# Hybrid attention, mixture-of-experts and linear-attention kernel: two steps of the first attention stage moved, both attention stages' layer loops written out

## The chip, the core and the metric

The kernel runs on one core of one Trainium2 chip. The metric is the device time of one execution in microseconds. Before the change it was 3831.24 us, the median of three runs (3824.48 to 3834.24).

## What the kernel computes

The input `x` has 8 sequences of 512 tokens with 128 channels, all in float32. Four stages follow one another, each applied to the normalised `x` and added to it:

```python
x = x + attn_a(layernorm(x))   # 16 heads of 64
x = x + ffn(layernorm(x))      # router, 16 experts of which 8 count per token, one shared expert
x = x + attn_b(layernorm(x))   # a transformer of 6 layers, 16 heads of 8, linear attention
x = x + ffn(layernorm(x))
```

Only `attn_a` and `attn_b` are touched. `attn_a`, cut to what matters:

```python
# per head; SK is a running sum of outer products that begins at eye * sqrt(64)
SK = cumsum(outer(kk, vk)) + SK_state
y  = q @ (SK / (norm(SK) + 1e-8)).T          # the new query
scores = rotary(y) @ rotary(k).T / 8         # causal, softmax over 512 keys
out = softmax(scores) @ v ; return concat_heads(out) @ w_out + b_out
```

`attn_b` runs six layers of projections, exponential feature maps, causal linear attention, an output projection, layer norm, a feed-forward of 512 and a second layer norm.

## The kernel before

Everything stays on chip: `x` is one tile of 128 partitions by 8 x 512. In the attention stage a "layer" is one of 8 pairs of heads; within a layer the 8 sequences go through one after the other. Work on a sequence is a list of named steps, and three sequences are in flight at once: one comes in (projections, states, the new query), one is mixed (scores, softmax, weighing), one goes out. A *slot* is one turn of this pipeline: all steps of `AttentionPlan.SLOT` (line 216), once. `LEAD` and `FIRST` are shorter lists that fill the pipeline, `TAIL` and `END` empty it.

Each engine walks the same slots by the function `pipeline` (line 168) and issues only what it has to do in each step. TensorE and GpSimd take the order of `SLOT`; ScalarE and VectorE have orders of their own (`ACT`, `DVE`, lines 218 and 219). Each engine executes its queue strictly in order. Between engines there are counters: a matmul group that fills a PSUM bank raises `filled[bank]`, the engine that has read it raises `emptied[bank]`. `FILLS` (line 220) says which banks a step fills; `Slot.fill` computes from the order of the steps which count a wait must reach. There are eight banks: a0, a1, a2 for the incoming sequence, s0, s1 for scores, t0, t1 for turned probabilities, z for the weighed sum.

The steps that matter here, with TensorE's line and who reads the result:

- P0, P3 (line 445): projections of q and vk, of k and kk, into a0 and a1; ScalarE copies them (lines 622, 632).
- P1, P2 (line 445 too, as 128x384): the token projections of chunks 0 and 1 (banks a2, a0) and 2 and 3 (a1, a2). ScalarE copies them to `tok[parity_in]` (line 627). This buffer also holds the values which W3 of the same slot reads.
- L0, L1 (line 485): linear scores of the first and the second half, into a0 and a1; VectorE masks them (line 692). L1 needs P3's banks, so ScalarE's copies of `k_own` and `kkT`, to be done.
- St (line 500): the state products, into a2; VectorE adds them up (line 702), after its part of S2.
- Yi (line 511) needs VectorE's masked scores, Ys (line 518) the added states; then ScalarE copies y (line 636), VectorE forms `zk` and its running sum, and `inc` (line 527) multiplies with it. `inc` is TensorE's last step of a slot.
- S0 to S3 (lines 557, 561): scores of query chunk c; VectorE takes the maximum, ScalarE the exponential (line 658).
- T0 to T3 (line 577): turn the probabilities; ScalarE copies them (line 647). W0 to W3 (line 590): weigh the values with them into bank z.
- `inv` (line 535) and `outs` (line 544): turned reciprocals, and the output projection.

The transformer stage is built in the same way from `TransformerPlan`, with slots that begin with the turn of `o` (line 1019) and end with S1, 64 small matmuls (line 977).

The layers run in a loop. `e.Fori` emits its body once and jumps back at its end; inside, counts to wait for depend on the layer, so they are computed by register instructions. The attention stage loops over 7 of its 8 layers and the transformer over 5 of its 6; the last layer is emitted by itself. SyncE's own loop of the transformer's weight loads, and the loops of the `ffn` stages, are separate.

Of the kernel before, what the change touches and what calls it, by code (L numbers as in the profile page):

```python
# [134 lines left out]
def fills(plan, steps, bank):  # L135

    return sum(plan.FILLS[step].split().count(bank) for step in steps)


class Slot:  # L140
# [20 lines left out]
    def fill(self, bank, step):  # L161

        plan = self.plan
        n = sum(fills(plan, p, bank) for p in self.passed) + fills(plan, self.steps[:self.steps.index(step)], bank)
        return self.slots * fills(plan, plan.SLOT, bank) + n


def pipeline(e, plan, weights_in, weights_out, body, order=None):

    def run(slot, sequence):
        for step in slot.steps if order is None else [step for step in order if plan.joins(step, slot.steps)]:
            if step != "weights":
                body(step, slot, sequence)
            elif slot.build is not None:
                weights_in(slot.build, slot)

    B, once = plan.B, [plan.LEAD, plan.FIRST]  # L180
    weights_in(0, None)
    run(Slot(plan, plan.LEAD, [], 0, 0, 0, 0, new_weights=True), {"in": 0, "next": 1})
    run(Slot(plan, plan.FIRST, once[:1], 0, 0, 0, 0), {"in": 1, "next": 2})

    def layer(l, final):
        g = l * B

        def slot(z, parity, **more):
            return Slot(plan, plan.SLOT, once, g + (z - 1), g + z, l, parity, **more)

        weights_out(l, slot(1, 1, final=final))
        for z in range(1, B - 2):
            run(slot(z, z % 2), {"in": z + 1, "next": z + 2, "out": z - 1})
        run(slot(B - 2, 0, build=None if final else l + 1), {"in": B - 1, "next": B, "out": B - 3})
        if final:
            run(Slot(plan, plan.TAIL, once, g + (B - 2), g + (B - 1), l, 1), {"out": B - 2})
            run(Slot(plan, plan.END, once + [plan.TAIL], g + (B - 2), g + B, l, 0), {"out": B - 1})
        else:
            run(slot(B - 1, 1, new_weights=True), {"in": 0, "next": 1, "out": B - 2})
            run(slot(B, 0), {"in": 1, "next": 2, "out": B - 1})  # L200

    with e.Fori(0, plan.LAYERS - 1) as l:
        layer(l, False)
    layer(plan.LAYERS - 1, True)


def sequence_of(tokens, z):
# [3 lines left out]
class AttentionPlan:  # L211
# [1 line left out]

    SLOT = ("P0 T3 S0 W3 P1 inv P2 S1 L0 outs T0 P3 weights T1 L1 Xn S2 St W0 W1 Yi Ys T2 S3 W2 inc").split()
    LEAD = "X P0 P1 P2 L0 P3 L1 Xn St Yi Ys inc".split()
    ACT = "P0 T3 S0 P1 inv P2 S1 T0 P3 T1 S2 Ys T2 S3".split()
    DVE = "W3 S0 inv S1 L0 outs P3 weights L1 S2 St Ys S3 inc rot scale".split()
# [1 line left out]
                 Ys="a0 a1", inc="a2", inv="t0", outs="a2", T0="t0", weights="", T1="t1", T2="t0 t1", T3="t0 t1",  # L221
# [4 lines left out]
    END = "T3 W3 inv outs".split()  # L226
    FIRST = [step for step in SLOT if step not in ("T3", "W3", "inv", "outs")]
    TAIL = [step for step in SLOT if step[0] in "STWio" and step not in ("St", "inc")]

# [5 lines left out]
def attention_block(nc, mem, ins, B):  # L235
# [12 lines left out]
    plan = AttentionPlan()  # L248
    plan.B, plan.LAYERS = B, PAIRS
    with ExitStack() as ctx:  # L250
# [3 lines left out]
        def sem(name):  # L254
            return ctx.enter_context(nc.semaphore("a_" + name))
# [41 lines left out]
        filled = {k: sem("filled_" + k) for k in plan.BANKS}  # L297
# [14 lines left out]
        def wait(e, name, slot, n):  # L312

            e.wait_ge(s[name], slot.of(PHASE[name]) * EVENTS[name] + (n + 1))

        def wait_filled(e, bank, slot, step):
            e.wait_ge(filled[bank], slot.fill(bank, step) + 2)
# [9 lines left out]
        def wait_staged(e, hp, slot, step=None):  # L327

            e.wait_ge(w_loaded, (hp + 1) * 16)
            if slot is not None:  # L330
                for bank in ("a0", "a1", "a2"):
                    e.wait_ge(filled[bank], slot.fill(bank, step or slot.steps[0]) + 1)
            e.nop(nofuse=True)
# [4 lines left out]
        with nc.Block() as block:  # L338
            @block.sync
            def _(sp):  # L340
# [20 lines left out]
                def body(step, slot, sequence):  # L361
# [3 lines left out]
                    elif step == "Ys":  # L365
                        wait_emptied(sp, "a0", slot, "Ys")
                        swap(y_swap, y_own, s["y_swapped"])

                pipeline(sp, plan, weights_in, weights_out, body)
                sp.wait_ge(mem["rest_loaded"], mem["rest_loads"])  # L370
                sp.wait_ge(w_loaded, PAIRS * 16)
# [51 lines left out]
            def _(pe):  # L423
# [9 lines left out]
                def body(step, slot, sequence):  # L433
# [147 lines left out]
                    elif step[0] == "W":  # L581
# [13 lines left out]
                        if c == TILES - 1:  # L595
                            t.then_inc(filled["z"], 1)

                pipeline(pe, plan, weights_in, weights_out, body)

            @block.scalar  # L600
            def _(act):
                for k in plan.BANKS:
                    act.sem_inc(emptied[k], 1)
                act.sem_inc(made_out, 1)

                def weights_in(hp, slot):
                    pass

                def weights_out(hp, slot):
                    wait_staged(act, hp, slot)  # L610
                    nc.scalar.copy(w_o[:], staged[:, 5 * P:6 * P]).then_inc(made_out, 1)
                    act.wait_ge(made_out, hp + 2)
                    act.nop(nofuse=True)

                def body(step, slot, sequence):
                    def full(bank):
                        wait_filled(act, bank, slot, step)

                    if step == "P0":
                        for n in range(2):  # L620
                            full(f"a{n}")
                            nc.scalar.copy(qv[:, :, n, :], ps[f"a{n}"].rearrange("p (c n) -> p c n", c=TILES)
                                           ).then_inc(emptied[f"a{n}"], 1)
                    elif step in ("P1", "P2"):
                        for n, bank in enumerate(plan.FILLS[step].split()):
                            full(bank)
                            nc.scalar.copy(tok[slot.parity_in][:, 2 * (step == "P2") + n, :],
                                           ps[bank][:, 0:3 * P]).then_inc(emptied[bank], 1)
                    elif step == "P3":
                        for dst, bank in ((k_own, "a0"), (kkT, "a1")):  # L630
                            full(bank)
                            nc.scalar.copy(dst[:], ps[bank]).then_inc(emptied[bank], 1)
                    elif step == "Ys":
                        full("a0")
                        full("a1")
                        nc.scalar.copy(y_own[:].rearrange("p (c n) -> p c n", c=TILES), yz[:, :, 0, :]
                                       ).then_inc(emptied["a0"], 1)
                    elif step == "inv":
                        full("t0")
                        nc.scalar.copy(inv_rows[:], ps["t0"][:]).then_inc(emptied["t0"], 1)  # L640
                    elif step[0] == "T":
                        c = int(step[1])
                        n, banks = (c + 1) * P, plan.FILLS[step].split()
                        for i, bank in enumerate(banks):
                            hs = slice(0, 2) if len(banks) == 1 else slice(i, i + 1)
                            full(bank)
                            nc.scalar.copy(probT[c % 2][:, hs, 0:n],  # L647
                                           ps[bank][:, 0:2 * n // len(banks)].rearrange("p (h n) -> p h n", n=n)
                                           ).then_inc(emptied[bank], 1)
                    elif step[0] == "S":  # L650
                        c = int(step[1])
                        wait(act, "shifts", slot, c + 1)
                        if c == 0:
                            act.wait_ge(s["inv"], slot.of("mix") + 1)
                            act.nop(nofuse=True)
                        for h in range(2):
                            k = 2 * c + h
                            nc.scalar.activation(prob[c % 2][h][:, 0:(c + 1) * P], ps[f"s{h}"][:, 0:(c + 1) * P],  # L658
                                                 ACT.Exp, bias=shift[:, k:k + 1], scale=scale[slot.parity][:, k:k + 1],
                                                 accum_out=row_sum[:, k:k + 1]).then_inc(emptied[f"s{h}"], 1)  # L660

                pipeline(act, plan, weights_in, weights_out, body, plan.ACT)

            @block.vector
# [94 lines left out]
class TransformerPlan:  # L759


    SLOT = ("turn att project values Wo mapq A1 mapk h1 keys weights F1 sums S0 F2 nums A0 S1").split()
    LEAD = "turn project values mapq mapk keys sums S0 A0 S1".split()
# [6 lines left out]
                 S0="s0 s1 s2 s3", S1="s0 s1 s2 s3", A0="n0", A1="n1",  # L770
# [1055 lines left out]
```

## Time and profile before

| | |
|---|---|
| median of 3 runs | 3831.24 us (3824.48 to 3834.24) |
| the profiled execution's own time | 3831.35 us |
| its span, first to last instruction | 3829.6 us |
| instructions | 103815 |
| TensorE matmuls busy | 3485.5 us, 91% |
| TensorE weight loads busy | 2723.9 us, 71% |
| VectorE busy | 2636.2 us, 69% |
| ScalarE busy | 1703.6 us, 44% |
| GpSimd busy | 901.5 us, 24% |
| mean granted TensorE clock | 0.972 |

The attention stage lies between about 50 and 1600 us, the transformer stage between about 1980 and 3460 us; the two `ffn` stages follow them. A busy share is the time in which an engine had an instruction in work. In a row of waits, "A <- B" says that the engine named first stood idle until B released it; "issue" stands for idle time in which it waited for nothing that the profile shows. Matmul durations overlap, so the step from start to start counts, not the sum of durations.

### The profile page before, as it was taken

Reading aid. Unit: us, or ns where it says so; the run is one execution under the profiler, and the core shown is the slowest. Engines: PE = TensorE matmul, PEld = TensorE weight load, DVE = VectorE, ACT = ScalarE, POOL = GpSimd, SP = SyncE. Lnnn points to the kernel's source line nnn. Section 1 sums busy time; section 2 is a strip of 40 time slices with the busy share of each in tenths; the row PEclk is TensorE's granted clock in tenths of the full one; section 3 lists DMA queues with packets and bytes.
Section 4 is the critical chain, followed back from the end, with each engine's and each line's share of the span. In section 5 each row is a group of like instructions: output and inputs, shape, how many; then the busy total and the mean of one; then the engine's idle time right before and its main releaser. Section 6 shows DMA issues by size and latency. Waiting matters only on the chain. (4 is left out here: it accounts for less than half of the span.)

```text
span 3829.6 us, 103815 instructions
## 1 busy us (share of the span) xinstructions
PE 3485.5 (91%) x39640; PEld 2723.9 (71%) x39640; DVE 2636.2 (69%) x6838; ACT 1703.6 (44%) x3438; POOL 901.5 (24%) x781
## 2 busy tenths in 40 slices
PE   4999999999999999799958999999999999987998
PEld 3767676767676777688846777777777777756887
DVE  3565655555655555588866778878888788867787
ACT  2555555555555555433323444444434444422332
POOL 3232323232323232100001332232223222320000
PEclk9999999999999999899979999999999999988999
DMA  3000000000000000000000000000000000000000
GB/s 88 29 24 28 24 28 24 28 24 28 24 28 24 28 23 23 12 1 0 1 14 16 2 16 2 2 16 2 16 3 2 16 2 3 2 2 1 1 0 22
DMA packets 38420, 60.41 MB, mean 16 GB/s; under 512 B 6960, under 2 KB 16688, under 8 KB 37552
## 3 DMA queue, kind: packets, MB, share of 16 engines
q1 hardware_dynamic: 37936, 53.78, 4.3%
q8 instruction: 326, 5.34, 0.6%
q14 instruction: 158, 1.29, 0.1%
HBM read 18.10 MB, written 2.10 MB: 5 GB/s over the span
## 5 line engine op out<-in xcount | busy, mean ns | idle before, releaser
L658 ACT ACTIVATE a_prob<-a_s,a_shift,a_scale 128x128 f32<-128x128 f32 (+3 forms) x512 | 311.5, 612 | 483.6 <-DVE a_shift L741 483.4
L1538 ACT ACTIVATE ffn_silu<-ffn_ps_g 128x512 f32<-128x512 f32 x272 | 161.2, 599 | 382.5 <-PE ffn_ps_g L1488 370.2
L1481 PEld LDWEIGHTS ffn_ps_y<-moe_down,ffn_hidden 128*128 128x128 f32 x2176 | 282.1, 191 | 40.0 <-issue 18.5
L1481 PE MATMUL ffn_ps_y<-moe_down,ffn_hidden 128*128 128x128 f32 x2176 | 288.1, 275 | 16.0 <-DVE ffn_acc L1642 16.0
L940 POOL TENSOR_TENSOR t_rstd<-t_var_eps,minus_half 128x4 f32<-128x4 f32 x96 | 97.7, 1017 | 834.9 <-DVE t_var_eps L1252 834.9
L1190 ACT COPY t_num<-t_n 128x512 f32<-128x512 f32 x96 | 56.2, 585 | 515.4 <-PE t_n L1001 514.8
L1642 DVE SCALAR_TENSOR_TENSOR ffn_acc<-ffn_ps_y,ffn_combine,ffn_acc 128x128 f32<-128x128 f32 x960 | 270.5, 347 | 7.7
L1654 DVE TENSOR_TENSOR ffn_hidden<-ffn_silu,ffn_ps_u 128x512 f32<-128x512 f32 x272 | 186.1, 686 | 106.5 <-ACT ffn_silu L1538 74.5
L409 POOL TENSOR_TENSOR a_k_sin<-a_k_swap,sin_swap 128x512 f32<-128x512 f32 x64 | 81.7, 1277 | 721.6 <-DMA a_k_swap<-a_k_own 721.6
L738 DVE TENSOR_REDUCE a_neg_max<-a_s 128x2 f32<-128x256 f32 (+3 forms) x256 | 208.8, 816 | 59.9 <-PE a_s L561 56.7
L1327 DVE TENSOR_TENSOR t_mixed<-t_s,upto 128x512 f32<-128x512 f32 x384 | 238.4, 684 | 14.5 <-PE t_s L977 12.4
L692 DVE TENSOR_TENSOR a_lin<-a_a,lin_mask 128x512 f32<-128x512 f32 x256 | 165.0, 686 | 78.5 <-PE a_a L485 78.5
L977 PE MATMUL t_s<-t_phi_q,t_kz 32*128 32x64 f32 x6144 | 205.4, 274 | 13.0 <-issue 11.0
L590 PE MATMUL a_z<-a_probT,a_tok 128*64 128x128 f32 x2560 | 179.8, 278 | 39.6 <-ACT a_probT L647 39.5
L577 PE MATMUL a_t<-ident,a_prob 128*128 128x128 f32 x1280 | 203.9, 284 | 7.8 <-ACT a_prob L658 4.2
L557 PE MATMUL a_s<-a_keys,a_query 64*128 64x128 f32 (+3 forms) x1024 | 205.1, 474 | 2.5 <-issue 2.1
L977 PEld LDWEIGHTS t_s<-t_phi_q,t_kz 32*128 32x128 f32 x6144 | 188.5, 186 | 25.3 <-issue 18.3
L577 PEld LDWEIGHTS a_t<-ident,a_prob 128*128 128x128 f32 x1280 | 150.9, 144 | 66.4 <-issue 49.0
L1001 PE MATMUL t_n<-t_mixed,t_v_pad 128*32 128x64 f32 x6144 | 185.1, 223 | 7.3 <-DVE t_mixed L1327 7.3
L647 ACT COPY a_probT<-a_t 128x512 f32<-128x512 f32 (+2 forms) x384 | 188.2, 528 | 6.6 <-PE a_t L577 4.5
L1117 PE MATMUL t_s<-t_oT,t_w 128*128 128x512 f32 x384 | 182.6, 619 | 8.5 <-ACT t_oT L1196 1.7
L750 DVE TENSOR_TENSOR a_headsT<-a_z,a_inv_rows 128x512 f32<-128x512 f32 x64 | 44.3, 692 | 206.9 <-ACT a_inv_rows L640 206.9
(209 smaller groups left out, 8813.1 us busy)
## 6 DMA issues: line engine op xcount, KB each, us to landing
a_k_swap<-a_k_own SPq DMA_DIRECT2D x128, 128.0 KB, 2.1
a_y_swap<-a_y_own SPq DMA_DIRECT2D x128, 128.0 KB, 2.0
a_staged<-in_pairs SPq DMA_DIRECT2D x8, 384.0 KB, 3.1
t_next<-in_t_w SPq DMA_DIRECT2D x12, 256.0 KB, 3.1
t_next_rows<-in_t_rows SPq DMA_DIRECT2D x6, 448.0 KB, 4.1
x<-in_x SPq DMA_DIRECT2D x8, 256.0 KB, 4.5
out<-x SPq DMA_DIRECT2D x1, 2048.0 KB, 8.7
t_next_sq<-in_t_sq SPq DMA_DIRECT2D x6, 256.0 KB, 2.6
```

The lines of the kernel that those rows point to most:

```text
L557: nc.tensor.matmul(ps[f"s{h}"][:, 0:(c + 1) * P], query[slot.parity][rows(h), own], keys[slot.parity][rows(h), 0:(c + 1) * P], start=True, ...
L577: t = nc.tensor.transpose(ps[bank][:, (at + j) * P:(at + j + 1) * P], prob[c % 2][h][:, j * P:(j + 1) * P], mem["ident"][:])
L647: nc.scalar.copy(probT[c % 2][:, hs, 0:n], ps[bank][:, 0:2 * n // len(banks)].rearrange("p (h n) -> p h n", n=n)).then_inc(emptied[bank], 1)
L658: nc.scalar.activation(prob[c % 2][h][:, 0:(c + 1) * P], ps[f"s{h}"][:, 0:(c + 1) * P], ACT.Exp, bias=shift[:, k:k + 1], scale=scale[slot. ...
L738: nc.vector.tensor_reduce(neg_max[:, two], ps_s[:, :, 0:(c + 1) * P], AX.X, ALU.max, negate=True).then_inc(s["negs"], 1)
L977: mm = nc.tensor.matmul(ps[f"s{r}"][:, u * SPAN:(u + 1) * SPAN], kz[t][strip(r), u, :, :].rearrange("p h n -> p (h n)"), phi_q[parity][t][ ...
L1001: mm = nc.tensor.matmul(ps[bank][strip(r), at], v_pad[:, u, 4 * t + r, :, :].rearrange("p h n -> p (h n)"), mixed[t][r][:, u, :], start=u ...
L1117: nc.tensor.matmul(ps[f"s{f}"][:], w_1[:, chunk(f)], h1T[:], start=True, stop=True).then_inc(filled[f"s{f}"], 1)
L1327: nc.vector.tensor_tensor(mixed[t_][r][:], ps[f"s{r}"][:].rearrange("p (u n) -> p u n", u=SPANS), mem["upto"][:].unsqueeze(1).broadcast_to ...
L1481: t = nc.tensor.matmul(ps_y[e % 2][:, c * P:(c + 1) * P], hidden[e % 3][:, c * P:(c + 1) * P], w_down[:, e * P:(e + 1) * P], start=True, s ...
L1642: t = nc.vector.scalar_tensor_tensor(acc[:, c, :], y, combine[parity][:, c, e:e + 1], acc[:, c, :], ALU.mult, ALU.add)
L1654: nc.vector.tensor_tensor(hidden[e % 3][:], silu[e % 2][:], ps_u[e % 2][:], ALU.mult).then_inc(hid_done, 1)
```

## The change

The order of TensorE's (and GpSimd's) steps changes in two places: P1 stands ahead of W3, and St ahead of L1, where it stood behind S2. The orders of ScalarE and VectorE stay. Because ScalarE's copies of P1 overwrite the values that W3 reads, and W3 now comes after P1, ScalarE waits in P1 until W3 has filled bank z. `layer` is called eight and six times with numbers, so the loops disappear from every engine that walks the pipeline; the counts to wait for become constants.

```diff
--- before.py
+++ after.py
@@ -199,9 +199,8 @@
-    with e.Fori(0, plan.LAYERS - 1) as l:
-        layer(l, False)
-    layer(plan.LAYERS - 1, True)
+    for l in range(plan.LAYERS):
+        layer(l, l == plan.LAYERS - 1)
@@ -213,7 +212,7 @@
-    SLOT = ("P0 T3 S0 W3 P1 inv P2 S1 L0 outs T0 P3 weights T1 L1 Xn S2 St W0 W1 Yi Ys T2 S3 W2 inc").split()
+    SLOT = ("P0 T3 S0 P1 W3 inv P2 S1 L0 outs T0 P3 weights T1 St L1 Xn S2 W0 W1 Yi Ys T2 S3 W2 inc").split()
@@ -622,6 +621,10 @@
                     elif step in ("P1", "P2"):
+                        if step == "P1":
+
+                            act.wait_ge(filled["z"], slot.fill("z", "P2") + 1)
+                            act.nop(nofuse=True)
                         for n, bank in enumerate(plan.FILLS[step].split()):
                             full(bank)
```

## Rows read from the trace of the kernel before

**Rows 1.** Waits, 60 to 1585 us; engine line <- awaited: us, times, longest
```profile
PE a_z L590 <- ACT a_probT L647: 38.7, 55, 1.3
...
PE a_a L485 <- ACT a_kkT L632: 21.5, 64, 0.8
...
PE a_a L445 <- issue: 19.5, 6, 3.5
```

**Rows 2.** Timeline, TensorE, one slot; start, us, engine line, operands, count, [idle before]
```profile
1002.63 1.05 PE L527 MATMUL a_a<-twos_own,a_zk_upto 128*128 128x2 f32 x8
...
1007.54 1.09 PE L590 MATMUL a_z<-a_probT,a_tok 128*64 128x128 f32 x16 [0.70 <-ACT a_probT L647]
...
1011.94 1.11 PE L485 MATMUL a_a<-a_qv 64*128 64x256 f32 x8
...
1016.52 1.13 PE L485 MATMUL a_a<-a_qv 64*128 64x256 f32 x8 [0.33 <-ACT a_kkT L632]
...
1018.31 0.57 PE L500 MATMUL a_a<-a_tok 128*64 128x64 f32 x12
1018.71 0.83 PE L590 MATMUL a_z<-a_probT,a_tok 128*64 128x128 f32 x12
1019.37 1.90 PE L511 MATMUL a_a<-a_lin,a_tok 128*64 128x256 f32 x16
1021.20 1.95 PE L518 MATMUL a_a<-a_qv,a_state 64*64 64x256 f32 x16
...
1025.87 1.05 PE L527 MATMUL a_a<-twos_own,a_zk_upto 128*128 128x2 f32 x8
```

**Rows 3.** Timeline, ScalarE, the same slot
```profile
1009.40 1.01 ACT L627 COPY a_tok<-a_a 128x384 f32<-128x384 f32 x2 [0.58 <-PE a_a L445]
```

**Rows 4.** Timeline, VectorE, the same slot
```profile
1017.66 1.29 DVE L692 TENSOR_TENSOR a_lin<-a_a,lin_mask 128x512 f32<-128x512 f32 x2 [1.25 <-PE a_a L485]
...
1020.20 0.48 DVE L702 TENSOR_TENSOR a_state<-a_a,a_state 128x64 f32<-128x64 f32 x2
```

**Rows 5.** Timeline, TensorE, `inc` before and after a loop's jump
```profile
283.66 1.05 PE L527 MATMUL a_a<-twos_own,a_zk_upto 128*128 128x2 f32 x8
...
311.83 1.05 PE L527 MATMUL a_a<-twos_own,a_zk_upto 128*128 128x2 f32 x8
```

**Rows 6.** Windows, around that jump; window, length, busy by engine, clock, DMA
```profile
284.00:292.00 8.00, 4.90 (x20) 4.15 (x20) 3.54 (x9) 3.49 (x8) 2.40 (x2) 0.69 0.21 58
```

**Rows 7.** Timeline, TensorE, `inc` where the loop ends and the last layer begins
```profile
1430.87 1.05 PE L527 MATMUL a_a<-twos_own,a_zk_upto 128*128 128x2 f32 x8
...
1454.63 1.05 PE L527 MATMUL a_a<-twos_own,a_zk_upto 128*128 128x2 f32 x8
...
1478.03 1.05 PE L527 MATMUL a_a<-twos_own,a_zk_upto 128*128 128x2 f32 x8
```

**Rows 8.** Waits, transformer stage, 1977 to 3455 us
```profile
PE t_w L1019 <- issue: 12.1, 4, 3.4
...
PE t_s L977 <- issue: 11.0, 24, 1.0
```

**Rows 9.** Waits, written-out last layer, 3258 to 3400 us
```profile
PE t_s L977 <- issue: 1.2, 2, 0.7
```

**Rows 10.** Timeline, TensorE, first instruction of six transformer slots
```profile
2488.54 0.65 PE L1019 MATMUL t_w<-ident,t_o_now 128*128 128x128 f32 x4
...
2551.46 0.66 PE L1019 MATMUL t_w<-ident,t_o_now 128*128 128x128 f32 x4
...
2638.95 0.66 PE L1019 MATMUL t_w<-ident,t_o_now 128*128 128x128 f32 x4
...
3200.18 0.65 PE L1019 MATMUL t_w<-ident,t_o_now 128*128 128x128 f32 x4
...
3258.59 0.66 PE L1019 MATMUL t_w<-ident,t_o_now 128*128 128x128 f32 x4
...
3345.01 0.81 PE L1019 MATMUL t_w<-ident,t_o_now 128*128 128x128 f32 x4
```

## The prediction

> **What bounds the kernel now.** I read the busy shares first (the table of the profile above): TensorE has work for 91% of the span, so what counts is where it stands still. The other engines are at 24 to 69%, and none of them is the bound over a stage. I then asked for the waits of the first attention stage alone, and took TensorE's rows [rows 1]. Three groups stand out. W3 (line 590, the last weighing) waits for ScalarE's copies of the turned probabilities: 38.7 us in 55 waits. L1 (line 485, second linear scores) waits for ScalarE's copy of kk: 21.5 us in 64 waits. P0 (line 445) waits six times for nothing that the profile shows: 19.5 us, and six is the number of times that a loop over seven layers jumps back. Each of the three is touched by one of the edits.
>
> Then one slot in order of time, TensorE [rows 2], ScalarE [rows 3], VectorE [rows 4]. The reader is to see TensorE packed from row to row except for 0.70 us before W3 and 0.33 us before L1. From one `inc` (line 527) to the next is 1025.87 - 1002.63 = 23.24 us.
>
> **Edit 1: P1 ahead of W3.** P1 is six matmuls of 384 columns, 0.16 us each at 2.4 GHz, so with their weight loads about 1.1 us; it needs banks a2 and a0, which `inc` and P0's copies gave back earlier. So it fills the 0.70 us. W3's copies are done when W3 starts at 1007.54 today; in the new order it would start at 1007.54 - 0.70 + 1.1 = 1007.94, 0.40 later than they allow. The wait goes whole: 38.7 us, less about 1.5 in the two closing slots, which have no P1, is 37. In the six slots after a jump the wait is absent today because TensorE comes late; once the jump goes (below) they would have had it, so 6 x 0.70 = 4 more. Sum 41.
>
> What it adds: ScalarE's P1 copies now wait for W3's end (bank z), since they overwrite the values that W3 reads. Behind that wait on ScalarE stand the copies `inv`, P2, then S1's exponentials. W3's end would be near 1007.94 + 1.09 = 1009.03, and the P1 copies start near 1009.15, where they start at 1009.40 today [rows 3]. So they come 0.25 us earlier while TensorE comes 0.70 earlier: 0.45 us of slack is used up. Who waits for them: P2's second group (bank a2), which TensorE reaches about 0.9 us after W3's end, behind `inv` and P2's first group, against some 0.6 for the wait and one copy; and L0 (line 485, at 1011.94 today), which wants a1, emptied by the fourth copy of about 0.5 us each, so near 1011.15 against a wish for 1011.24. I allow 0.05 us per slot. Bounds: nothing if the wait is as quick as others, 0.4 if the extra wait and no-op cost ScalarE that much in dispatch.
>
> **Edit 2: St ahead of L1.** St takes 1018.71 - 1018.31 = 0.40 us [rows 2], more than L1's 0.33 us wait; a2 was freed by `outs` before. VectorE still takes St's bank after its S2 step, so nothing is produced for it earlier: the edit only fills the hole. 21 us. What is late next: Yi (line 511) comes 1.03 us earlier in all, and wants the second lin product, which starts with L1's first result [rows 4]: 1017.66 + 1.29 = 1018.95, shifted by 0.63 (0.70, less the 0.07 that St is longer than the wait) to 1018.32, against Yi's wish 1019.37 - 1.03 = 1018.34. A tie. Ys (line 518) wants the state sums: 1020.20 + 0.48 = 1020.68, less 0.63 is 1020.05, against 1021.20 - 1.03 = 1020.17. Near tie. I allow 0.05 us again. Together the two allowances are 0.1 x 62 slots = 6 us. Bounds for both: 0 and 0.5 us a slot (31 us), half of what is gained.
>
> From Ys to the next P0 nothing is moved: VectorE's zk, the scan and the query keep their distance to Ys.
>
> **Edit 3: loops written out, attention stage.** Across a jump a slot lasts 311.83 - 283.66 = 28.17 us [rows 5], 4.93 more than 23.24. The issue gap is 19.5 / 6 = 3.25 of it; the rest is clock: over the 8 us around this jump the granted clock is 0.69 on average [rows 6], so TensorE is at 1.2 GHz for the larger part of it after having stood idle. The kernel already holds one change of layer without a jump, where the loop ends and the last layer, written out, begins: 1454.63 - 1430.87 = 23.76, and the slot after it 1478.03 - 1454.63 = 23.40 [rows 7]. So a jump is worth (28.17 - 23.24) - (23.76 - 23.40) = 4.57 us, six times 27. Straight slots are 0.16 us longer than loop slots; most of that stands in the W3 wait, which is now covered, so I charge 2 us (bounds 0 and 0.16 x 62 = 10). The register instructions that go away cost TensorE nothing here, since its queue runs ahead.
>
> Sum of the stage: -41 - 21 + 6 - 27 + 2 = -81 us.
>
> **Edit 3, transformer stage.** Four jumps, 12.1 us of gap, 3.0 on average [rows 8]. Two slots around a jump take 2551.46 - 2488.54 = 62.92 us; the same two where the loop ends take 3258.59 - 3200.18 = 58.41 [rows 10]. That is 4.5 us for a jump whose gap is 3.4; less 0.4 for the average one, 4.1, four times 16. The rest of the 32 slots: three loop slots take 2638.95 - 2551.46 = 87.49, 29.16 each; three straight ones 3345.01 - 3258.59 = 86.42, 28.81 each. The difference of 0.35 is the balance of two things: register work gone, and stalls with no releaser in S0 and S1 (line 977: 11.0 us in 24 [rows 8]), short bursts of 64 small matmuls, where I take instructions to arrive late. They occur in the written-out layer too: 1.2 us in two of some five slots [rows 9], about as often as in the loop. Three slots are few, and stalls could fall thicker elsewhere, so I take less than half, 0.15 x 32 = 5 us (bounds: 0.35 the other way, +11, and 0.35 with the 11.0 us of stalls gone as well, -22). Sum -21.
>
> One rule of the Trainium skill speaks on this: "Runtime: NRT & Kernel Launch", section Instruction fetch mechanics, says that a taken branch outside the fetched window stalls, and that crossing into the next block in straight code is mostly hidden. On the jump this trace agrees (3.25 us). On straight code it shows stalls all the same. What the stage would do by the rule is the first rival.
>
> **Total.** The profiled execution took 3831.35 us, the median of the runs is 3831.24, so both are one figure. 3831 - 81 - 21 = 3729 us, 2.7% faster.
>
> **Rivals.**
> No stalls in straight code: the full 0.35 x 32 = 11 us instead of 5, and the 11.0 us of line 977 gone as well, 17 us more: 3712 us. For it: 96 such steps show 24 stalls, most show none, so where it falls may hang on the jumps. Against: the two in the written-out layer. By the page named above this would be the case. Chance 0.14.
> The holes move instead of closing: P1's copies, Yi or Ys come late, because three near ties stand in a row. Half of the 62 us lost: 3760; all of it: 3791, where only the loops' gain is left. For it: margins of 0.02 to 0.12 us. Against: each tie broken costs only its own excess. Chance 0.18.
> Slower than before: TensorE outruns its instructions. With holes and jumps gone there is no pause in which the supply catches up, and every slot, of the 62 and the 40, stalls in its bursts. It decides from 102 us over 102 slots, 1.0 us a slot more than today; at 1.3 us the time is 3729 + 133 = 3862. For it: 24 stalls, the longest 1.0 us. Against: attention's straight slots (23.40) show nothing like it. Chance 0.05.
> Nothing changes: 0.01. The edits certainly remove the jumps, so I see no way to it but a chance balance.
>
> **How the numbers follow.** The forecast, 0.62, is 3729. Low end: the no-stall rival less a few microseconds, 3703. High end: the forecast with the stage's small terms at their bad ends, and the first half of the second rival: 3729 + 31 = 3760, and a little over, 3765. Left out are the rest of the second rival and the slow one. About 0.3% can be told from no change. Faster 0.93, same 0.02, slower 0.05.
>
> **What would show it.** Right: waits of line 590 for the turned probabilities only in two or three slots; none of line 485 for kk; no issue gaps before P0 or the turn of o (line 1019); `inc` to `inc` 22.3 to 22.4 us; granted clock 1.00 at changes of layer; the transformer's slots near 29. Wrong: new waits before Yi, Ys or L0 of over 0.2 us; line 977 with more than 20 us of issue; a slot of 23 us or more.

## The result, and the profile after

The changed kernel takes 3787.45 us (median of four runs, 3783.13 to 3792.82), the kernel before 3829.22 beside it: a ratio of 0.9887, 95% interval 0.9874 to 0.990. It is 1.1% faster, where 2.7% was forecast, and lies above the forecast's range. The profiled execution took 3792.82 us.

From the page of the profile after (engine, busy us, share of the span, instructions):

```profile
span 3791.1 us, 98421 instructions
...
PE 3495.8 (92%) x39640; PEld 2727.7 (72%) x39640; DVE 2686.2 (71%) x6838; ACT 1684.5 (44%) x3438; POOL 902.1 (24%) x781
```

VectorE is 50 us busier than before (2636.2), though it was given nothing to do. That is the first hint.

The stage by stage account comes from the timelines: the first to the last `inc` for attention, the first to the last turn of `o` for the transformer. Attention went from 1498.5 to 1466.6 us (-31.9, forecast -81), the transformer from 1387.25 to 1375.84 (-11.4, forecast -21); the span is 38.5 shorter, so 5 us were given back in the rest of the kernel, which no edit touches.

The waits of the attention stage after, 60 to 1545 us (engine line <- awaited: us, times, longest), answer to [rows 1]:

```profile
PE a_a L517 <- DVE a_state L705: 42.0, 52, 0.9
...
ACT a_tok L630 <- PE a_z L589: 24.7, 59, 0.7
...
PE a_a L484 <- ACT a_kkT L635: 0.8, 1, 0.8
```

All three groups of [rows 1] are gone: none of W3's (line 589 now) and none of issue before P0 is left, of L1's one. In their place stands one that the kernel before did not have: Ys (line 517) waits in 52 slots, 42.0 us, for the added states. Before, it waited 1.1 us in two. (The other line is ScalarE's new wait for bank z. It costs ScalarE 0.4 us a slot; no wait of TensorE goes back to it.)

One slot after, TensorE, answers to [rows 2]:

```profile
1005.39 1.05 PE L526 MATMUL a_a<-twos_own,a_zk_upto 128*128 128x2 f32 x8
...
1010.71 1.09 PE L589 MATMUL a_z<-a_probT,a_tok 128*64 128x128 f32 x16
...
1018.17 0.57 PE L499 MATMUL a_a<-a_tok 128*64 128x64 f32 x12
1018.67 1.13 PE L484 MATMUL a_a<-a_qv 64*128 64x256 f32 x8
...
1020.46 0.88 PE L589 MATMUL a_z<-a_probT,a_tok 128*64 128x128 f32 x12
1021.26 1.95 PE L510 MATMUL a_a<-a_lin,a_tok 128*64 128x256 f32 x16
1024.04 1.94 PE L517 MATMUL a_a<-a_qv,a_state 64*64 64x256 f32 x16 [0.82 <-DVE a_state L705]
...
1028.76 1.05 PE L526 MATMUL a_a<-twos_own,a_zk_upto 128*128 128x2 f32 x8
```

W3 (1010.71) and L1 (1018.67) start without a wait, as forecast, and still the slot takes 1028.76 - 1005.39 = 23.37 us. (W3 starts 5.32 us into the slot against 4.91 before, 0.41 later; 0.40 was forecast.) Yi starts 15.87 us into the slot, 0.87 earlier than before (16.74); Ys starts 18.65 into it, 0.08 later (18.57). All that was won up to Yi is lost between Yi and Ys.

What VectorE and GpSimd do just then, in the same slot after:

```profile
1020.50 1.28 POOL L408 TENSOR_TENSOR a_k_sin<-a_k_swap,sin_swap 128x512 f32<-128x512 f32 x1 [10.12 <-DMA a_k_swap<-a_k_own]
1021.03 0.95 DVE L741 TENSOR_REDUCE a_neg_max<-a_s 128x2 f32<-128x768 f32 x1
...
1021.95 1.27 POOL L412 TENSOR_TENSOR a_keys<-a_k_cos,a_k_sin 128x512 f32<-128x512 f32 x1 [0.17 <-POOL a_k_sin L408]
1022.02 1.22 DVE L744 TENSOR_TENSOR a_shift<-a_neg_max,a_scale 128x2 f32<-128x2 f32 x1
...
1023.40 0.48 DVE L705 TENSOR_TENSOR a_state<-a_a,a_state 128x64 f32<-128x64 f32 x2
```

and in the kernel before, in the slot of [rows 2 to 4]:

```profile
1019.84 0.16 DVE L741 TENSOR_TENSOR a_shift<-a_neg_max,a_scale 128x2 f32<-128x2 f32 x1
1019.89 1.27 POOL L413 TENSOR_TENSOR a_keys<-a_k_cos,a_k_sin 128x512 f32<-128x512 f32 x1 [0.17 <-POOL a_k_sin L409]
```

`shift` is the smallest instruction of VectorE's S2 step: two columns, a maximum times a scale, both from SBUF. It takes 0.16 us before and 1.22 after. What differs is who is first: before it starts 0.05 us ahead of GpSimd's `keys`, after it 0.07 behind. Behind `shift` VectorE has the state sums in its queue, and Ys waits for these.

### The profile page after: what moved, and what is told of

Its sections match the earlier page's. It is cut to its first block and busy times, and to the rows that moved or that the text cites. A ratio compares the mean times of both kernels' runs of the same rounds, so it can differ in the third digit from the quotient of the medians.

```text
span 3791.1 us, 98421 instructions
## 1 busy us (share of the span) xinstructions
PE 3495.8 (92%) x39640; PEld 2727.7 (72%) x39640; DVE 2686.2 (71%) x6838; ACT 1684.5 (44%) x3438; POOL 902.1 (24%) x781
## 5 line engine op out<-in xcount | busy, mean ns | idle before, releaser
L416 POOL TENSOR_TENSOR a_norm<-a_norm,plus_half 128x8 f32<-128x8 f32 x64 | 125.4, 1959 | 305.8 <-DVE a_norm L719 305.8
L1128 PE MATMUL t_w<-t_w,t_hid 128*128 128x128 f32 x1536 | 184.2, 278 | 2.1 <-DVE t_hid L1361 2.1
```

Source lines behind the costliest of these rows:

```text
L1128: t = nc.tensor.matmul(ps["w1"][:, chunk(c)], hid[f][:, chunk(c)], w_2[:, f, :], start=f == 0, stop=f == FT - 1)
```

## The experiments

Theory A, formed from these rows: `shift` can't run while GpSimd works on `keys`, and the second edit made it lose the race. Theory B: there is no lock. The moved steps only bring TensorE up against VectorE's chain of work, which sets Ys's start whatever `shift` does. A third possibility is that the place of P1 or of St costs time by itself. All times are medians; ratios are to the kernel before in runs beside them. That kernel took 3829.22 us beside after, 3834.38 beside unroll_only, no_st, no_p1 and sums_early, 3839.48 beside pool_later, cliff, shift_scalar and turn_first, and 3839.37 beside the last four, so kernels of different groups are compared by ratio or by stage. "Slot" is the median from `inc` to `inc`, "long" the number of `shift` over 1 us.

| kernel | us | ratio [95%] | attention stage | slot | long | Ys waits for states, us |
|---|---|---|---|---|---|---|
| before | 3829.22 | 1 | 1498.5 | 23.23 | 2 | 1.1 |
| after | 3787.45 | 0.9887 [0.9874, 0.990] | 1466.6 | 23.38 | 51 | 42.0 |
| unroll_only | 3802.71 | 0.9919 [0.9903, 0.9936] | 1477.5 | 23.39 | 1 | 0.6 |
| no_st | 3755.25 | 0.9792 [0.9774, 0.9811] | 1428.4 | 22.62 | 0 | none |
| no_p1 | 3843.13 | 1.0024 [1.0013, 1.0034] | 1513.7 | 24.15 | 50 | 39.6 |
| sums_early | 3753.00 | 0.9789 [0.9773, 0.9805] | 1424.2 | 22.50 | 45 | none |
| pool_later | 3795.50 | 0.9883 [0.9858, 0.9908] | 1464.7 | 23.36 | 48 | 39.8 |
| cliff | 3760.96 | 0.9799 [0.9781, 0.9817] | 1427.4 | 22.60 | 0 | none |
| shift_scalar | 3758.06 | 0.9797 [0.9780, 0.9813] | 1430.4 | 22.68 | 0 | none |
| turn_first | 3739.68 | 0.9748 [0.9731, 0.9764] | 1424.7 | 22.51 | 44 | none |
| pool_later2 | 3749.17 | 0.9756 [0.9740, 0.9772] | 1422.7 | 22.51 | 0 | 0.7 |
| cliff2 | 3794.39 | 0.9878 [0.9861, 0.9894] | 1465.0 | 23.37 | 47 | 33.6 |
| loops_kept | 3833.66 | 0.9984 [0.9974, 0.9993] | 1490.3 | 23.36 | 39 | 32.9 |
| sums_first | 3743.21 | 0.9751 [0.9734, 0.9767] | 1427.9 | 22.52 | 43 | none |

### The three edits one by one

**unroll_only**: the loops written out, both steps where they were (the slot's order of before, no wait in P1).

```diff
-    SLOT = ... T3 S0 P1 W3 inv ... T1 St L1 Xn S2 W0 ...
+    SLOT = ... T3 S0 W3 P1 inv ... T1 L1 Xn S2 St W0 ...
-                            act.wait_ge(filled["z"], slot.fill("z", "P2") + 1)
```

> The loops written out, both steps at their old places. Theory A (a lock between VectorE and GpSimd: with St ahead of L1 the tiny product `shift` of S2 comes just behind the start of GpSimd's `keys` and stands for its 1.2 us, so St's move costs 0.8 us a slot and P1's move gains 0.8): slots of 23.4 us as in the written-out layer before, total near 3788, as the changed kernel. Theory B (no lock: the moves only bring TensorE up against VectorE's chain, each gains nothing once the other is there): also near 3788. This run fixes the share of the loops for both.

**no_st**: the change with St back behind S2.

```diff
-    ... T0 P3 weights T1 St L1 Xn S2 W0 W1 Yi Ys T2 S3 W2 inc
+    ... T0 P3 weights T1 L1 Xn S2 St W0 W1 Yi Ys T2 S3 W2 inc
```

> The changed kernel with St back behind S2; P1 ahead of W3 and the loops written out stay. Theory A: L1 comes 0.1 us earlier behind k_own's copy, the product `shift` of S2 slips in between GpSimd's two instructions, lasts 0.16 us again, and Ys has no wait: slots of 22.5 to 22.6 us, total near 3743. Theory B: VectorE's chain sets Ys either way, slots stay at 23.4, total 3785 to 3800.

**no_p1**: the change with P1 back behind W3, and without ScalarE's wait for bank z.

```diff
-    SLOT = P0 T3 S0 P1 W3 inv ...
+    SLOT = P0 T3 S0 W3 P1 inv ...
-                            act.wait_ge(filled["z"], slot.fill("z", "P2") + 1)
```

> The changed kernel with P1 back behind W3 (without ScalarE's wait for bank z); St ahead of L1 and the loops written out stay. Theory A: the stretch from T1 to Ys is as in the changed kernel, so `shift` of S2 lasts 1.2 us and Ys waits 0.8: slots of 24.2 us, total near 3832, slower than unroll_only by some 45 us. Theory B: St's move gains its 0.33 us or nothing: total 3765 to 3788.

The second edit alone costs time, with either order of P1: from unroll_only to no_p1 the attention stage grows by 36.2 us (the kernel by 40), from no_st to after by 38.2 (the kernel by 36, from the ratios). The first edit gains 49.1 us of the stage (unroll_only to no_st). Writing out the loops gains 21.0. In no_st, where St is back, the race is won again (its timeline, the same columns as above):

```profile
1019.29 0.16 DVE L744 TENSOR_TENSOR a_shift<-a_neg_max,a_scale 128x2 f32<-128x2 f32 x1
1019.34 1.27 POOL L412 TENSOR_TENSOR a_keys<-a_k_cos,a_k_sin 128x512 f32<-128x512 f32 x1 [0.17 <-POOL a_k_sin L408]
```

P1's place has no part in it: no_p1 has 50 long `shift` instructions and 39.6 us of waits. Theory B had the slots of no_st at 23.4 us, and they take 22.62. What is left beside the lock is that St's place costs time by itself.

The slots came as theory A had them (23.4, 22.5 to 22.6, 24.2), the totals 11 to 15 us above it: 3802.71 against 3788, 3755.25 against 3743, 3843.13 against 3832. A part of that may be the drift of the kernel before, 5 us slower beside these runs. For unroll_only both theories had 3788, the time of the changed kernel, and both missed: the two moves don't cancel, they are worth -49.1 + 38.2 = -10.9 us of the stage together.

**sums_early**: VectorE takes St's bank ahead of L1, so that the sums no longer stand behind `shift`.

```diff
-    DVE = "W3 S0 inv S1 L0 outs P3 weights L1 S2 St Ys S3 inc rot scale".split()
+    DVE = "W3 S0 inv S1 L0 outs P3 weights St L1 S2 Ys S3 inc rot scale".split()
```

> The changed kernel with VectorE's St step (the three state sums) ahead of L1 instead of behind S2, in VectorE's idle time before L1. Theory A: `shift` of S2 still stands behind GpSimd's `keys`, but only ScalarE's exponentials of S2 wait for it, and T2 needs them later; Ys has no wait: slots of 22.5 us, total near 3745, a few us lost in the eight slots with new weights. Theory B: Ys is released by the same chain of VectorE, shortened by some 0.9 us: also a gain, 3745 to 3765. What tells them apart here is the length of `shift` in the trace: over 1 us by A, 0.16 by B.

From the timeline of sums_early:

```profile
1020.21 1.26 POOL L412 TENSOR_TENSOR a_keys<-a_k_cos,a_k_sin 128x512 f32<-128x512 f32 x1 [0.17 <-POOL a_k_sin L408]
1020.27 1.23 DVE L744 TENSOR_TENSOR a_shift<-a_neg_max,a_scale 128x2 f32<-128x2 f32 x1
```

`shift` is as long as in the changed kernel, in 45 slots, and the slot is 22.50 us all the same. Theory B wanted a `shift` of 0.16 us here. So the long `shift` costs time only through the sums queued behind it; it is not a consequence of anything that they do. (The total was forecast near 3745 us and came at 3753.00.)

### The race itself

**pool_later**: four no-ops on GpSimd ahead of `keys`, to let `shift` win.

```diff
+                        for _ in range(4):
+                            pool.nop(nofuse=True)
                         nc.gpsimd.tensor_tensor(keys[slot.parity_in][:], k_cos[:], k_sin[:], ALU.add).then_inc(s["keys"], 1)
```

> The changed kernel with four no-ops on GpSimd ahead of `keys`, some 0.1 to 0.3 us. Theory A: work is added, nothing is taken away, yet `shift` of S2 now starts ahead of `keys` and lasts 0.16 us; Ys has no wait, slots near 22.5, total 3748 to 3756, 35 us faster than the changed kernel. If no-ops take less than 0.1 us, part of the slots still collide. Theory B: no change or a little slower, 3787 to 3795.

It did not move what it was to move: `keys` starts 0.17 us after `k_sin` as before, the no-ops are hidden behind `k_sin`. As a test it says nothing. But its timeline holds two neighbouring slots that differ by less than 0.1 us in who is first:

```profile
998.80 1.27 POOL L414 TENSOR_TENSOR a_keys<-a_k_cos,a_k_sin 128x512 f32<-128x512 f32 x1 [0.17 <-POOL a_k_sin L408]
998.88 1.20 DVE L746 TENSOR_TENSOR a_shift<-a_neg_max,a_scale 128x2 f32<-128x2 f32 x1
...
1022.26 0.16 DVE L746 TENSOR_TENSOR a_shift<-a_neg_max,a_scale 128x2 f32<-128x2 f32 x1
1022.27 1.29 POOL L414 TENSOR_TENSOR a_keys<-a_k_cos,a_k_sin 128x512 f32<-128x512 f32 x1 [0.17 <-POOL a_k_sin L408]
```

**pool_later2**: the same with work that can't be hidden, a memset of 128x128 on GpSimd ahead of `keys`.

```diff
+                        nc.gpsimd.memset(idle[:], 0.0)
                         nc.gpsimd.tensor_tensor(keys[slot.parity_in][:], k_cos[:], k_sin[:], ALU.add).then_inc(s["keys"], 1)
```

> The changed kernel with a memset (128x128) on GpSimd ahead of `keys`, because the no-ops of pool_later were hidden (`keys` followed 1.44 us behind `k_sin` as before). Theory A: if `keys` starts over 0.1 us later, `shift` starts ahead of it and lasts 0.16 us: work is added and the total falls to 3750 to 3760. Rival B: no change or slower, 3787 to 3800.

From the timeline of pool_later2, GpSimd and VectorE:

```profile
1039.48 0.20 POOL L413 MEMSET a_idle<- 128x128 f32 x1
1039.58 0.16 DVE L746 TENSOR_TENSOR a_shift<-a_neg_max,a_scale 128x2 f32<-128x2 f32 x1
1039.65 1.27 POOL L414 TENSOR_TENSOR a_keys<-a_k_cos,a_k_sin 128x512 f32<-128x512 f32 x1
```

An instruction is added to every slot, and the attention stage is 43.9 us shorter than the changed kernel's; by the ratios the kernel is 1.3% faster. In 47 slots `shift` starts within the memset, which writes and does not read, and takes 0.16 us all the same. In 13 others it starts within `k_sin` and takes 0.16 to 0.87 us: it waits for the rest of `k_sin`. (The total, 3749.17, is 1 us below the range of theory A.)

**cliff** and **cliff2**: the reverse. In no_st, where `shift` wins, a memset on VectorE ahead of S2's maximum, of 128x8 and of 128x256.

```diff
+        idle = sb("idle", [P, 8])          # cliff2: [P, 256]
...
+                        if c == 2:
+                            nc.vector.memset(idle[:], 0.0)
                         nc.vector.tensor_reduce(neg_max[:, two], ...
```

> no_st (St at its old place, 3755 us) with one tiny VectorE instruction (a memset of 128x8) ahead of S2's maximum. There `shift` starts 0.05 us ahead of `keys`. Theory A: the 0.1 us is enough to bring it behind; `shift` lasts over 1 us, Ys waits about 0.4 to 0.8, total 3785 to 3800. Theory B: the instruction costs what it takes, at most 0.1 x 62 = 6 us: 3755 to 3762.

> As cliff, with a larger memset (128x256, about 0.25 us), because the small one was hidden and moved `shift` by 0.02 us only, so that it still started ahead of `keys`. Theory A: `shift` now starts after `keys`, ends with it (1.28 to 1.30 us after its start), Ys waits 0.6 to 0.8 us; slots 23.3 to 23.4, total 3795 to 3805. Rival B: the delay costs what it takes, at most 0.25 x 62 = 16 us: 3761 to 3777.

In cliff the memset took 0.07 us and for the most part overlapped the end of the masking product in front of it; `shift` starts 0.01 us later than in no_st, still 0.038 us ahead of `keys` (median), and nothing happens. So cliff decides nothing. The timeline of cliff2:

```profile
1019.71 0.27 DVE L743 MEMSET a_idle<- 128x256 f32 x1
...
1020.66 1.27 POOL L413 TENSOR_TENSOR a_keys<-a_k_cos,a_k_sin 128x512 f32<-128x512 f32 x1 [0.17 <-POOL a_k_sin L409]
1020.82 1.12 DVE L747 TENSOR_TENSOR a_shift<-a_neg_max,a_scale 128x2 f32<-128x2 f32 x1
```

With St where it was, and the order of TensorE's steps that of the fast kernel, a memset of 0.27 us makes the stage 36.6 us longer, over twice the 0.25 x 62 = 16 us of the rival, and the stage takes as long as the changed kernel's within 2 us. St's place is not what costs, then, except through the race.

**shift_scalar**: the product `shift` of all four score steps written as two instructions, each with one tensor and one column as a per-partition scalar.

```diff
-                        nc.vector.tensor_tensor(shift[:, two], neg_max[:, two], scale[slot.parity][:, two],
-                                                ALU.mult).then_inc(s["shifts"], 1)
+                        for h in range(2):
+                            k = 2 * c + h
+                            t = nc.vector.tensor_scalar(shift[:, k:k + 1], neg_max[:, k:k + 1],
+                                                        scale[slot.parity][:, k:k + 1], None, ALU.mult)
+                        t.then_inc(s["shifts"], 1)
```

> The changed kernel with `shift` formed by two tensor_scalar instructions, each with one tensor operand and a scalar per partition, in place of one tensor_tensor with two. Theory A, if the lock is for instructions that read two tensors from SBUF: no long `shift`, slots near 22.6 (0.1 for the second instruction), total 3755 to 3765. Rival: any VectorE instruction on SBUF stands behind GpSimd's: the wait stays, 3790 to 3800.

From the timeline of shift_scalar:

```profile
1020.76 1.27 POOL L408 TENSOR_TENSOR a_k_sin<-a_k_swap,sin_swap 128x512 f32<-128x512 f32 x1 [11.01 <-DMA a_k_swap<-a_k_own]
...
1021.47 0.33 DVE L746 TENSOR_SCALAR a_shift<-a_neg_max,a_scale 128x1 f32<-128x1 f32 x2
```

Both are done in 0.33 us in the middle of `k_sin`, and none of 512 in the kernel takes over 0.22 us, though the median start still is 0.07 us behind `keys`. So it hangs on the instruction and not on VectorE as a whole: two tensor operands of two columns are held up, one column beside a scalar isn't.

One tensor operand is not safe in every shape, though. The transformer stage, in every version, has a product of one tensor (128x512) with a per-partition scalar, and GpSimd's work beside it. From the timeline of after:

```profile
2232.11 1.28 POOL L951 TENSOR_TENSOR t_scaled<-t_xn,t_rows 128x512 f32<-128x512 f32 x1 [1.30 <-DVE t_xn L1262]
2232.77 3.10 DVE L1285 TENSOR_SCALAR t_kz<-t_phi_k,strip_head 128x512 f32<-128x512 f32 x4 [0.80 <-ACT t_phi_k L1189]
2233.53 1.27 POOL L954 TENSOR_TENSOR t_h1b<-t_scaled,t_be_bf 128x512 f32<-128x512 f32 x1
```

The four products take 0.90, 1.49, 0.47 and 0.47 us. Of the 192 in this kernel 100 start while GpSimd is idle and take 0.47 to 0.49 us; the other 92 take 0.49 to 1.50 and end 0.28 us or more after GpSimd's instruction. They are held up too.

**loops_kept**: both moves in the kernel before, loops kept.

```diff
-    SLOT = ... T3 S0 W3 P1 inv ... T1 L1 Xn S2 St W0 ...
+    SLOT = ... T3 S0 P1 W3 inv ... T1 St L1 Xn S2 W0 ...
+                            act.wait_ge(filled["z"], slot.fill("z", "P2") + 1)
```

> Both moved steps with the loops kept: edits 1 and 2 alone. Theory A: the loop's slots meet the same lock (in the loop `shift` led `keys` by 0.06 us, St's move costs it more than that), so P1's 0.7 us are given back: slots near 23.3, total 3825 to 3845. Rival C: the lock needs the longer reaction times of the written-out code; in the loop `shift` still slips in and both moves pay: slots 22.3, total 3765 to 3780.

Together the moves are worth 0.16% in the loop, -8.2 us of the stage; the race is lost in 39 slots here too. The written-out counts are not its cause.

### What else stood between the forecast and the result

**turn_first**: sums_early, and in the transformer ScalarE copies `o` for TensorE's turn first, and the outgoing weights of the next layer behind it.

```diff
+                due = []
                 def weights_out(l, slot):
+                    due.append((l, slot))
+                def take_weights(l, slot):
                     wait_staged(act, l, slot)
...
                                        sequence_of(mem["o"], sequence["in"])).then_inc(s["o_now"], 1)
+                        if due:
+                            take_weights(*due.pop())
                         full("w0")
```

> sums_early (3753 us) with one edit in the transformer stage: at a change of layer ScalarE copies `o_now` first and its outgoing weights behind it. Theory: of the loop's jump only the issue gap went; TensorE still stands 1.4 us before the turn of `o`, because ScalarE's weight copies wait for the slot before, and its clock falls at each change of layer. Then five gaps of 1.4 us and the slow clock behind them go: 12 to 20 us, total 3735 to 3741. Rival: the clock falls for other reasons (the stalls in S1) and only the gaps go: 3746 to 3750.

The transformer stage goes from 1379.3 to 1362.1 us. The waits of its first TensorE instruction, line 1022, in sums_early, and then in turn_first:

```profile
PE t_w L1022 <- ACT t_o_now L1170: 47.5, 7, 38.8
```

```profile
PE t_w L1022 <- ACT t_o_now L1175: 39.6, 1, 39.6
```

Six waits of some 1.4 us at changes of layer go, 8.7 us. The rest of the 17 is put down to the clock, which no longer falls at a change of layer. The stage as one window (start to end, length, busy and count of PE, PEld, DVE, ACT, POOL, granted clock, DMA share, GB/s) in sums_early, and in turn_first:

```profile
1920.00:3299.00 1379.00, 1318.16 (x22317) 1009.25 (x22320) 1097.19 (x2817) 599.06 (x964) 383.43 (x325) 0.98 0.02 7
```

```profile
1917.00:3279.00 1362.00, 1304.39 (x22310) 1001.09 (x22312) 1097.94 (x2820) 598.47 (x965) 384.63 (x326) 0.99 0.02 7
```

This is the lowest ratio of all kernels here, 0.9748; those of sums_first and pool_later2 lie within its interval.

**sums_first**: turn_first, with VectorE's part of St ahead of `weights` too.

```diff
-    DVE = "... P3 weights St L1 S2 Ys S3 inc rot scale".split()
+    DVE = "... P3 St weights L1 S2 Ys S3 inc rot scale".split()
```

> turn_first (3740 us) with VectorE's St step ahead of the building of new weights instead of behind it. It only matters in the seven slots that build weights, where Yi waits for the masked scores of L1 (4.8 us in 8 waits in sums_early): the weights then come behind the sums, the scores no earlier, so 0 to 3 us faster, 3736 to 3740.

3743.21 us, above the 3736 to 3740 expected; ratio 0.9751 against 0.9748, intervals that overlap: no gain. The few waits of Yi for the linear products grew from 4.8 to 8.2 us.

## Why the prediction was wrong

**Edit 1, P1 ahead of W3: right.** The waits go (one or two remain), the slots after a jump included, and the new wait on ScalarE delays nobody. Forecast 41 less 3 allowed; measured 49.1 with the loops written out. The surplus is the wait itself: it had grown in straight code, from 37.9 us in 54 (0.70 each) to 55.4 in 62 (0.89 each). Why each grew is not shown.

**Edit 2, St ahead of L1: the step that failed.** The prediction has it in the words "What is late next": Yi and Ys, two near ties, 0.05 us allowed for each pair. It moved VectorE's row of the state sums rigidly, "1020.20 + 0.48 = 1020.68, less 0.63", with everything in front of it. That is true of the times at which VectorE can start; but `shift`, between the maximum and the sums, had 0.05 us of lead on `keys`, and what it loses with that is not 0.05 us but the 1.1 us of `keys`. Against GpSimd VectorE comes 0.12 us later (median start of `shift` against `keys` -0.053 in no_st, +0.070 in after): the second linear product now starts after St, while GpSimd's `keys` hangs on ScalarE's copy of k and its transfer, which did not move. The margins that I did compute (0.02 for Yi, 0.12 for Ys) were of the size that I said, and harmless: in sums_early and pool_later2 Ys waits 0.7 us or less in all. The price is 0.82 in the slot shown, 42.0 in all, and the stage loses 38.2 instead of gaining 18.

The second rival comes to this sum ("all of it: 3791, where only the loops' gain is left"; measured 3787), but not by its mechanism. It argued "each tie broken costs only its own excess", and its ties were those of TensorE with what it reads. The tie that broke stood between two other engines, and 0.07 us of excess cost 1.1.

Also mis-sized: the hole of 0.33 us. With the race won (pool_later2 against no_st) the edit is worth 22.62 - 22.51 = 0.11 us a slot, and not 0.33. St takes 1018.67 - 1018.17 = 0.50 us where it is now and 0.40 where it was [rows 2], and the weighings W0 and W1 behind it take 1021.26 - 1020.46 = 0.80 against 1019.37 - 1018.71 = 0.66. A step's length hangs on its neighbours, with whose matmuls and weight loads its own overlap in the timeline; I took St's as its own.

**Edit 3, attention stage: right.** Forecast 25 net, measured 21.0. No issue gap before P0 is left.

**Edit 3, transformer stage: mechanism right, jump mis-sized.** I had 4.1 us for each of four jumps, from one pair of slots at the loop's end, 58.41 us [rows 10]. The five such pairs after take 60.75 to 62.37, 61.7 in the mean; the four pairs at jumps took 62.4. So a jump is worth 0.7 us, and the one sample was a lucky one: the same pair takes 3.4 us more after. What I overlooked is the clock in it. In the kernel before, windows of 8 us around the turn at a jump have a granted clock of 0.68 to 0.81, that around the turn of my pair 1.00, though TensorE waits 1.49 us there; at the same place after it waits 1.55 us and the clock is 0.72. The windows, before and then after (the granted clock is the column behind POOL's):

```profile
3226.20:3234.20 8.00, 6.27 (x124) 4.80 (x113) 7.11 (x18) 4.12 (x9) 5.36 (x6) 1.00 0.02 5
3185.50:3193.50 8.00, 6.12 (x75) 4.60 (x72) 6.51 (x16) 2.79 (x7) 5.63 (x6) 0.72 0.01 4
```

Why it did not fall in that one pair is not shown. At all five changes of layer after, the gap of the jump is gone and the fall of the clock is not (0.68 to 0.81 around the turn), where I had 1.00 forecast. TensorE waits 1.4 us for ScalarE there, which stands at its copies of the next layer's weights until the S1 of the slot before is over. From the timeline of after, ScalarE, then TensorE:

```profile
2485.80 0.30 ACT L1157 COPY t_w_o<-t_next_sq 128x128 f32<-128x128 f32 x1 [2.30 <-PE t_s L980]
2486.00 0.19 ACT L1158 COPY t_cols<-t_next_cols 128x6 f32<-128x6 f32 x1
2486.34 0.62 ACT L1170 COPY t_o_now<-o 128x512 f32<-128x512 f32 x1
...
2487.01 1.11 PE L1022 MATMUL t_w<-ident,t_o_now 128*128 128x128 f32 x4 [1.40 <-ACT t_o_now L1170]
```

The clock falls at such a change of layer (windows of 8 us, 36 us earlier and around it, both of after):

```profile
2448.00:2456.00 8.00, 6.68 (x204) 6.21 (x206) 7.03 (x24) 1.10 (x2) 1.44 (x2) 1.00 0.02 4
2484.00:2492.00 8.00, 6.60 (x63) 4.55 (x63) 5.60 (x12) 3.27 (x7) 5.32 (x5) 0.62 0.10 30
```

turn_first shows this by removing the wait: the clock is 1.00 around all five turns, and the pairs take 58.6 to 59.6 us. The steady slots gained more than the 5 us that I allowed: of the -11.4 us, -3 are the four jumps and +3.4 the pair at the loop's end, which leaves -12, near the 0.35 a slot of the three slots that I halved. The stalls of S1 stayed (9.7 us in 19 against 11.0 in 24 [rows 8]), which rules out the rival without stalls, and nothing of the slow rival appeared: P0, the turn and S1 have no more issue time than before.

Sum by the runs, attention: -21.0 - 49.1 + 38.2 = -31.9.

## What to carry to other kernels

A near tie is only harmless if both outcomes have been priced. When a step is moved by a tenth of a microsecond, list for each short VectorE instruction with two SBUF tensors which GpSimd instruction starts near it, and price the loss at that instruction's whole length for what is queued behind. Here one column with a per-partition scalar took the risk out, and so did a queue in which nobody waits behind the instruction; a 128x512 product with a scalar is held up as well, so the form has to be looked up in a trace. And a gain read from one sample is a guess: the five pairs of the changed kernel spread over 1.6 us.

## What the runs showed of the hardware

VectorE's 128x2 product of two SBUF tensors can't run beside GpSimd's 128x512 one once that has started. In the kernels with the original product, those that start ahead of `keys`, by as little as 0.000 us, last 0.16 us, or the rest of `k_sin` longer; the 360 that start 0.007 to 0.259 us behind it end 1.28 to 1.30 us after its start, without exception. The pause of 0.17 us between `k_sin` and `keys` is the door that `shift` went through in the kernel before. The other way round next to nothing is seen: `keys` lasts 1.26 to 1.30 us where it starts with `shift` still in work, and 1.26 to 1.28 where it doesn't.

The Trainium skill, "SBUF — State Buffer", section Who interferes with whom, has the rule: an instruction of VectorE with two SBUF inputs and one of GpSimd that reads SBUF share a read interface, and the second to start is blocked to the first's end. For `shift` behind GpSimd every run here agrees, the memset of pool_later2 too, which reads nothing and holds nothing up; that GpSimd is blocked in its turn no run here shows. The same section says that one SBUF input doesn't contend outside the 2-port perf modes. shift_scalar agrees for a column beside the scalar; the 128x512 product with a scalar (0.47 us alone, up to 1.50 beside GpSimd) does contend, and the traces don't tell an instruction's mode.

Four no-ops on GpSimd didn't move `keys`. A memset of 0.07 us on VectorE moved `shift` by 0.01 us, one of 0.27 us by 0.22 (from the end of the masking product, medians). Whether an added instruction shifts a race has to be read from its trace.
